# Attention scores from three bf16 parts in 32-wide tiles, with the masks of the transposed scores added by TensorE instead of selected by GpSimd

## The chip, the cores and the metric

The kernel runs on one core of a Trainium2 chip. The metric is the device time of one execution in microseconds, lower being better. The kernel before takes 4422.12 us (median of 3 runs, 4419.16 to 4424.13).

## The reference

One layer of a small language model over 32 sequences of 512 tokens, width 256, 16 heads of width 16. Every head attends twice: to keys at most 64 positions away, and to the first 64 keys of the sequence.

```python
h = take(emb_weight, x) + take(lora_A, x) @ lora_B.T * 2.0
n = layernorm(h)
q, k, v = split(n @ Wqkv + bqkv)                 # 16 heads of 16
s = q @ k.T / 4                                   # 512 x 512 of a head
attn_local  = softmax(where(abs(i - j) <= 64, s, -inf)) @ v
attn_global = softmax(q @ k[:64].T / 4) @ v[:64]
gate = sigmoid(n @ Wg + bg)
h = h + ((1 - gate) * attn_local + gate * attn_global) @ Wout + bout
n = layernorm(h)
# 8 experts, top 2 by softmax(n @ router_w.T), capacity 5121 rows of an expert
out = h + n + sum over the kept pairs of prob * (silu(n @ w1[e]) @ w2[e])
```

## The kernel before, in words

The program has a preparation, an attention stage (some 60 per cent of the time) and an expert stage, which the change leaves alone.

The attention stage goes through the sequences in turns. Turn i does the scores, exponentials and outputs of sequence i (`cur`), the projections of sequence i+1 (`nxt`), the embedding of i+2 (`far`), and the mixing, output projection and second layernorm of i-1 (`prev`); the routing of i-2 is in it too. Turns -2 to 3 and 30 to 34 are written out, turns 4 to 29 are one hardware loop (`turns`, L432). All engines follow one list of stages that `order` makes of 20 slots n = 0 to 19 and the tables `BEFORE` and `AFTER`; an engine skips the stages it has no part in, and each engine is in order.

A sequence has four quarters g of four heads, and each quarter five tiles: four of local scores (r = 0 to 3: a pair of heads by half a sequence) and one of global scores (r = 4). Slot n holds one tile of each of two kinds:

- `score_tile` (L715, L721) makes scores transposed, keys on partitions, queries along the row, in `psS[:, 0:2]`. ScalarE exponentiates them into `pl` or `pg` (L882, L886). GpSimd then sets what lies outside the band to zero (stage `sel`, L532 and L534), and `out_group` (L741, L746) multiplies by the values V.
- `max_tile` (L684, L696) makes scores the other way round in `psS[:, 2:4]`, adds the mask to them by a matmul of the identity with `mask` (L689), and VectorE takes the negated maxima of the rows (L970, L974) into `negm`. It works 9 slots ahead.

The maxima of a quarter go to `score_tile` as extra rows of Q against rows of ones in K, so that the subtraction is part of the matmul. Stage `m_rows` does that: TensorE transposes `negm` (L787), ScalarE and VectorE split it in two fp32r parts (L915, L1081), SyncE writes them to `m_scr` (L599), waits, and reads them into Q (L602). `score_tile` waits for this at the first tile of a quarter (slots 0, 5, 10, 15).

Precision comes from splitting: q and k are an fp32r high part and the rest (`qk_hi`, `qk_lo`, L941 and L1087), written three times to `qk_scr` (hi, lo, hi against hi, hi, lo), so one matmul contracts 48 rows, and two heads lie at partitions 0 and 64. SyncE's queue is in order too: in a turn it does load(i,3), m_rows(i,1), the load of `hb`, qk_write(i+1, 0), qk_write(i+1, 1) (L617), load(i+1,0) (L630), m_rows(i,2), load(i+1,1), m_rows(i,3), load(i+1,2), m_rows(i+1,0) and the stores of `held`, x2 and h. load(i+1,0) waits until all of qk_scr has landed.

## Time and profile before

| what | value |
|---|---|
| median of 3 runs | 4422.12 us |
| the profiled execution: time, span | 4414.52 us, 4412.8 us |
| share of the span that the engines are busy | PE 90%, DVE 56%, POOL 48%, ACT 41% |
| granted TensorE clock over the span | 0.902 of full speed |
| HBM read and written | 199.60 MB, 193.93 MB |

PE is TensorE's matmuls, PEld its weight loads, DVE VectorE, ACT ScalarE, POOL GpSimd, SP SyncE. The busy time of PE overlaps from one matmul to the next, since they are pipelined; what a group of matmuls costs is read from the start of the first to the start of what follows. A granted clock of 1.00 is 2.4 GHz, of 0.50 it is 1.2 GHz. An idle time stands with the work that ended it and what that work had waited for.

### The profile page before, as it was taken

Reading aid. Unit: us, or ns where it says so; the run is one execution under the profiler, and the core shown is the slowest. Engines: PE = TensorE matmul, PEld = TensorE weight load, DVE = VectorE, ACT = ScalarE, POOL = GpSimd, SP = SyncE. Lnnn points to the kernel's source line nnn. Section 1 sums busy time; section 2 is a strip of 40 time slices with the busy share of each in tenths; the row PEclk is TensorE's granted clock in tenths of the full one; section 3 lists DMA queues with packets and bytes.
Section 4 is the critical chain, followed back from the end, with each engine's and each line's share of the span. In section 5 each row is a group of like instructions: output and inputs, shape, how many; then the busy total and the mean of one; then the engine's idle time right before and its main releaser. Section 6 shows DMA issues by size and latency. Waiting matters only on the chain. (4 is left out here: it accounts for less than half of the span.)

```text
span 4412.8 us, 92560 instructions
## 1 busy us (share of the span) xinstructions
PE 3959.8 (90%) x31089; PEld 2974.9 (67%) x31090; DVE 2479.8 (56%) x5316; ACT 1830.4 (41%) x2933; POOL 2110.7 (48%) x2332
## 2 busy tenths in 40 slices
PE   2898989989989989998989987599999999999998
PEld 1455555555555555555555554599999999999998
DVE  3567676676677677667677674333343444334333
ACT  0344444444444444444444443344343444344343
POOL 2344555555555455455455444444444444444444
PEclk8798898898898898988888887799999999999999
DMA  5443443443443444444444431323232333322222
GB/s 125 99 130 101 113 131 92 113 129 101 105 128 102 111 122 106 126 103 113 121 100 113 126 97 41 98 46 65 46 68 45 65 58 56 64 46 48 44 44 41
DMA packets 243562, 395.27 MB, mean 90 GB/s; under 512 B 38533, under 2 KB 149589, under 8 KB 243317
## 3 DMA queue, kind: packets, MB, share of 16 engines
q1 hardware_dynamic: 170980, 301.18, 25.5%
q0 software_dynamic: 70512, 91.16, 12.0%
q8 instruction: 80, 1.31, 0.1%
q10 hardware_dynamic: 1952, 1.31, 0.1%
q14 instruction: 38, 0.30, 0.0%
HBM read 199.60 MB, written 193.93 MB: 89 GB/s over the span
## 5 line engine op out<-in xcount | busy, mean ns | idle before, releaser
L1344 POOL DMA_INDIRECT out_y<-out_t,tok_out x264 | 425.5, 1612 | 771.7 <-DMA out_y<-out_t,tok_out 410.0
L970 DVE TENSOR_REDUCE negm<-psS 128x4 f32<-128x1024 f32 x512 | 623.1, 1217 | 262.5 <-PE psS L689 260.0
L1552 DVE TENSOR_TENSOR h_lo<-act,h_hi 128x512 fp32r<-128x512 f32 x528 | 367.5, 696 | 583.5 <-ACT h_hi L1491 576.0
L1490 ACT ACTIVATE act<-psS 128x512 f32<-128x512 f32 x528 | 316.5, 600 | 911.0 <-PE psS L1418 899.1
L532 POOL TENSOR_SCALAR_AFFINE_SELECT pl<-pl 128x512 f32<-128x512 f32 x512 | 328.4, 641 | 757.6 <-ACT pl L882 757.3
L882 ACT ACTIVATE pl<-psS 128x896 f32<-128x896 f32 x512 | 468.3, 915 | 375.2 <-PE psS L715 373.0
L1453 PE MATMUL psO<-w_hi,h_hi 128*128 128x256 f32 x2112 | 598.9, 284 | 1.0 <-DVE h_lo L1552 0.9
L1453 PE MATMUL psO<-w_lo,h_hi 128*128 128x256 f32 x2112 | 588.8, 279 | 0.0
L1453 PE MATMUL psO<-w_hi,h_lo 128*128 128x256 f32 x2112 | 587.7, 278 | 0.0
L1418 PE MATMUL psS<-xg_hi,w_hi 128*128 128x256 f32 x1984 | 551.8, 278 | 0.1
L1418 PE MATMUL psS<-xg_hi,w_lo 128*128 128x256 f32 x1984 | 551.4, 278 | 0.0
L1418 PE MATMUL psS<-xg_lo,w_hi 128*128 128x256 f32 x1984 | 551.3, 278 | 0.0
L1453 PEld LDWEIGHTS psO<-w_hi,h_hi 128*128 128x128 f32 x2112 | 397.1, 188 | 1.6 <-DVE h_lo L1552 1.6
L1453 PEld LDWEIGHTS psO<-w_lo,h_hi 128*128 128x128 f32 x2112 | 397.0, 188 | 0.0
L1453 PEld LDWEIGHTS psO<-w_hi,h_lo 128*128 128x128 f32 x2112 | 395.5, 187 | 0.0
L1418 PEld LDWEIGHTS psS<-xg_hi,w_hi 128*128 128x128 f32 x1984 | 375.0, 189 | 0.3 <-issue 0.3
L1418 PEld LDWEIGHTS psS<-xg_lo,w_hi 128*128 128x128 f32 x1984 | 372.5, 188 | 0.0
L1418 PEld LDWEIGHTS psS<-xg_hi,w_lo 128*128 128x128 f32 x1984 | 372.5, 188 | 0.0
L715 PEld LDWEIGHTS psS<-Q,K 52*128 52x128 f32 x2048 | 171.5, 207 | 276.1 <-ACT pl L882 126.0
L689 PE MATMUL psS<-mask,identb 128*128 128x512 bf16 x1024 | 357.6, 436 | 0.0
L715 PE MATMUL psS<-Q,K 52*128 52x256 f32 (+1 forms) x2048 | 276.0, 351 | 76.9 <-ACT pl L882 59.0
L1584 DVE TENSOR_SCALAR out_t<-psO,wt_all 128x256 f32<-128x256 f32 x264 | 127.8, 484 | 367.8 <-PE psO L1453 362.9
(219 smaller groups left out, 7829.8 us busy)
## 6 DMA issues: line engine op xcount, KB each, us to landing
qk_scr<-qk_hi SPq DMA_DIRECT2D x128, 512.0 KB
Q<-qk_scr SPq DMA_DIRECT2D x256, 192.0 KB
K<-qk_scr SPq DMA_DIRECT2D x256, 192.0 KB
qk_scr<-qk_lo SPq DMA_DIRECT2D x64, 512.0 KB
h_rows<-held SPq DMA_DIRECT2D x32, 512.0 KB
hb<-h_rows SPq DMA_DIRECT2D x32, 512.0 KB
x_rows<-x SPq DMA_DIRECT2D x32, 512.0 KB
out_y<-h SPq DMA_DIRECT2D x32, 512.0 KB
```

Of the source, the lines that this page charges most:

```text
L532: pool.affine_select(out=cols[:, :, 0:P], in_=cols[:, :, 0:P], compare_op=ALU.is_ge, fill=0.0, base=0, pattern=[[0, 4], [1, P]], channel_m ...
L689: last = pe.matmul(psS[:, 2 + a, :], identb[:, :], mask[:, half, :, :], start=False, stop=True, skip_group_check=True)
L715: last = pe.matmul(psS[:, a, j % 2 * WIN + lo:j % 2 * WIN + hi], K[rows, 2 * g + v, j * P:(j + 1) * P], Q[rows, 2 * g + v, j * P - 64 + lo ...
L882: act.activation(pl[:, v, half, :, lo:hi], psS[:, 0:2, lo:hi], ACT.Exp, scale=SCALE).then_inc(exp_done, 1)
L970: dve.tensor_reduce(negm[:, g, 0, :, v, 2 * half:2 * half + 2], psS[:, 2:4, :].rearrange("p a (q u) -> p a q u", u=WIN), AX.X, ALU.max, ne ...
L1344: pool.indirect_dma_start(out=y[:, :], in_=out_t[:, tile.out, s, :], in_offset=None, out_offset=bass.IndirectOffsetOnAxis(ap=tok_out[:, ti ...
L1418: last = pe.matmul(psS[:, f // 2, (f % 2) * 256:(f % 2) * 256 + cols], w[:, tile.par, k, fs], x[:, k, 0:cols], start=(k == 0 and n == 0), ...
L1453: last = pe.matmul(psO[:, s, 0:D], h_[:, f, ts], w[:, tile.par, f, :], start=(f == 0 and n == 0), stop=(f == FT - 1 and n == 2))
L1490: act.activation(act32[:, b, :, 0:cols], src, ACT.Silu)
L1552: dve.tensor_tensor(h_lo[:, 2 * b:2 * b + 2, 0:cols], act32[:, b, :, 0:cols], h_hi[:, 2 * b:2 * b + 2, 0:cols].bitcast(F32), ALU.subtract) ...
L1584: dve.tensor_scalar(out_t[:, tile.out, s, :], psO[:, s, 0:D], wt_all[:, bass.ds(tile.h0 + s, 1)], None, ALU.mult).then_inc(out_done, 1)
```

## The change

q and k are cut in three bf16 parts instead of two fp32r ones: `qk1` by ScalarE, the rest in fp32 by VectorE, `qk2` by ScalarE (new stage `qk2`), `qk3` by GpSimd (new stage `qk3`). Six products of parts are kept, so a matmul contracts 96 rows and holds one head; with the maxima, in three parts also, 102 rows. The maxima are cut by VectorE before they are transposed (new stage `cut`), and m_rows comes later in its slot. Local scores are made in tiles of 32 rows of the result by 160 columns: each lands in 32 of the 128 PSUM partitions. `max_tile` adds the mask only where the band's corners are, and VectorE's maximum reads 160 columns of a block instead of 256. `score_tile` adds `mask_t` to the whole tile by matmuls with 32-wide pieces of the identity, and the stage `sel` of GpSimd is gone. The bias of the output projection is added in PSUM by one bf16 matmul per bank, and the copy `held` = h + bias on GpSimd is gone. Scratch takes about the same bytes in as many stores and half as many loads.

```diff
 # max_tile on TensorE
-                                lo, hi = edges(q)
                                 for a in range(2):
-                                    rows = slice(64 * a, 64 * a + ROWS)
-                                    pe.matmul(psS[:, 2 + a, q % 2 * WIN + lo:q % 2 * WIN + hi],
-                                              Q[rows, 2 * g + v, q * P:(q + 1) * P],
-                                              K[rows, 2 * g + v, q * P - 64 + lo:q * P - 64 + hi],
+                                    for c in range(4):
+                                        key = (4 * q + c) * SUB - SIDE
+                                        lo, hi = max(0, -key), min(BAND, T - key)
+                                        pe.matmul(psS[SUB * c:SUB * (c + 1), 2 + a, q % 2 * BAND + lo:q % 2 * BAND + hi],
+                                                  Q[0:ROWS, 4 * g + 2 * v + a, (4 * q + c) * SUB:(4 * q + c + 1) * SUB],
+                                                  K[0:ROWS, 4 * g + 2 * v + a, key + lo:key + hi],
...
-                                last = pe.matmul(psS[:, 2 + a, :], identb[:, :], mask[:, half, :, :], start=False, stop=True,
+                                for c in range(4):
+                                    last = pe.matmul(out[SUB * c:SUB * (c + 1), :, 0:5:4, :], identb[:, SUB * c:SUB * (c + 1)],
+                                                     tri[:, :, 0:5:4, :], start=False, stop=True, skip_group_check=True)
 # score_tile on TensorE
-                                    last = pe.matmul(psS[:, a, j % 2 * WIN + lo:j % 2 * WIN + hi],
-                                                     K[rows, 2 * g + v, j * P:(j + 1) * P],
-                                                     Q[rows, 2 * g + v, j * P - 64 + lo:j * P - 64 + hi],
-                                                     start=True, stop=True, skip_group_check=True)
+                                    for c in range(4):
+                                        key = (4 * j + c) * SUB
+                                        lo, hi = max(0, SIDE - key), min(BAND, T - key + SIDE)
+                                        pe.matmul(psS[SUB * c:SUB * (c + 1), a, j % 2 * WIN + SUB * c + lo:j % 2 * WIN + SUB * c + hi],
+                                                  K[0:ALL, 4 * g + 2 * v + a, key:key + SUB],
+                                                  Q[0:ALL, 4 * g + 2 * v + a, key - SIDE + lo:key - SIDE + hi],
+                                                  start=(j % 2 == 0), stop=False, skip_group_check=True)
+                            for j in range(2):
+                                for a in range(2):
+                                    for c in range(4):
+                                        pe.matmul(psS[SUB * c:SUB * (c + 1), a, j * WIN:j * WIN + SUB * (c + 1)],
+                                                  identb[:, SUB * c:SUB * (c + 1)], mask_t[:, 0:SUB * (c + 1)],
+                                                  start=False, stop=True, skip_group_check=True)
+                                    for c in range(4):
+                                        last = pe.matmul(psS[SUB * c:SUB * (c + 1), a, j * WIN + P + SUB * c:(j + 1) * WIN],
+                                                         identb[:, SUB * c:SUB * (c + 1)], mask_t[:, P + SUB * c:WIN],
+                                                         start=False, stop=True, skip_group_check=True)
 # out_group on TensorE
-                            pe.wait_ge(sel_done, SELECTS * s + 4 * g + 2 * (k + 1))
+                            pe.wait_ge(exp_done, JOBS * s + 5 * g + 2 * (k + 1))
 # GpSimd
-                            if stage == "sel":
...
-                                pool.affine_select(out=cols[:, :, 0:P], in_=cols[:, :, 0:P], compare_op=ALU.is_ge, fill=0.0,
...
+                            if stage == "qk3":
+
+                                pool.wait_ge(qk2_done, 4 * nxt + arg + 1)
...
+                                pool.tensor_tensor(qk3[:, arg, :], qk_rest[:, arg, :], qk2[:, arg, :], ALU.subtract).then_inc(qk3_done, 1)
 # SyncE, qk_write: each part of q (then of k) is waited for and written by itself
+                        for term, (rows, made) in enumerate(((qk1, qk1_done), (qk2, qk2_done), (qk3, qk3_done))):
+                            sp.wait_ge(made, 4 * s + 2 * (part + 1))
 # VectorE
-                            dve.tensor_reduce(negm[:, g, 0, :, v, 2 * half:2 * half + 2],
-                                              psS[:, 2:4, :].rearrange("p a (q u) -> p a q u", u=WIN),
+                            dve.tensor_reduce(negm[:, g, 0, v, :, 2 * half:2 * half + 2],
+                                              psS[:, 2:4, 0:2 * BAND].rearrange("p a (q u) -> p a q u", u=BAND),
 # the table AFTER, for one
-                5: (("cur", "out", 1), ("prev", "mix", 0), ("past", "top", 3)),
-                6: (("cur", "out", 2), ("prev", "mix", 1), ("past", "top", 4)),
+                5: (("cur", "out", 1), ("prev", "mix", 0), ("nxt", "qk3", 2), ("nxt", "qk3", 3), ("past", "top", 3)),
+                6: (("cur", "m_rows", 2), ("cur", "out", 2), ("prev", "mix", 1), ("past", "top", 4)),
```

How it moves instructions, at two places of the loop's turn. On TensorE, slot 6 before (the wait and transposes of m_rows(2), then a score tile and a max tile, then the output group and mixing):

```order
L787 MATMUL psX<-ident,negm 8x128 x4
L80 REGISTER_ALU
L715 MATMUL psS<-Q,K 128x192 x2
L715 MATMUL psS<-Q,K 128x256 x2
L684 MATMUL psS<-K,Q 128x192 x2
L684 MATMUL psS<-K,Q 128x256 x2
L689 MATMUL psS<-mask,identb 128x512 x2
L746 MATMUL psO<-pg,V 32x512 x4
```

and the same slot now, from the end of its score tile on; of that tile the last rows stand here. The numbers behind a name are partitions and columns of the result.

```order
L755 MATMUL psS<-mask_t,identb 32x32
L86 REGISTER_ALU
L702 MATMUL psS<-K,Q 32x96
L702 MATMUL psS<-K,Q 32x128
L702 MATMUL psS<-K,Q 32x160 x2
L702 MATMUL psS<-K,Q 32x96
L702 MATMUL psS<-K,Q 32x128
L702 MATMUL psS<-K,Q 32x160 x10
L709 MATMUL psS<-mask,identb 32x32 x2
L718 MATMUL psS<-mask,identb 32x2x2x32 x8
L825 REGISTER_ALU
L547 REGISTER_ALU
```

The score tile ahead of it went from 4 matmuls to 16 of scores (L744) and 32 of masks (L751, L755); the max tile went from 6 to 26; m_rows(2) (L828) now comes behind both. In one turn of the loop the program held 436 matmuls on TensorE before, and holds 1470 now.

On GpSimd, slots 5 and 6 before (`attn` is the sum of mix(0); the selections follow):

```order
L550 DMA emb_t<-in_L_tok_emb_weight,id_cur 128x256
L80 ISA
L566 ISA [waits attn_t_ready]
L567 TENSOR_TENSOR attn<-mix 128x256 [waits o_read]
L529 REGISTER_ALU
L532 AFFINE_SELECT pl<-pl 128x4x128 [waits exp_done]
L534 AFFINE_SELECT pl<-pl 128x4x128
```

and now (`qk<-qk_rest,qk` is qk3 from qk_rest and qk2):

```order
L573 DMA emb_t<-in_L_tok_emb_weight,id_cur 128x256
L86 ISA
L589 ISA [waits attn_t_ready]
L590 TENSOR_TENSOR attn<-mix 128x256 [waits o_read]
L594 REGISTER_ALU
L597 TENSOR_TENSOR qk<-qk_rest,qk 128x512 [waits qk2_done]
L594 REGISTER_ALU
L597 TENSOR_TENSOR qk<-qk_rest,qk 128x512 [waits qk2_done]
```

The last two cuts of k stand behind the sum of mix(0), which waits for VectorE's mixing; all of qk_write(i+1, 1) on SyncE waits for them.

## Rows read from the trace of the kernel before

**Rows 1.** Busy times in the loop of the attention stage and the expert stage

```profile
535.60:2585.00 2049.40, 1855.14 (x13911) 0.87 0.43 113
2830.00:4412.00 1582.00, 1532.38 (x13123) 0.98 0.30 54
```

**Rows 2.** TensorE at full clock: start, duration, engine, line, operation

```profile
1521.42 0.97 PE L696 MATMUL psS<-K,Q 48*128 48x64 f32 x16
1522.33 0.96 PE L741 MATMUL psO<-pl,V 128*32 128x256 f32 x16
1523.22 1.99 PE L773 MATMUL psX<-wv_sb,xn_t 128*128 128x256 f32 x8
...
1525.59 0.50 PE L715 MATMUL psS<-Q,K 52*128 52x192 f32 x4
1525.92 0.40 PE L684 MATMUL psS<-K,Q 48*128 48x192 f32 x4
1526.25 0.60 PE L689 MATMUL psS<-mask,identb 128*128 128x512 bf16 x2
1526.79 0.64 PE L746 MATMUL psO<-pg,V 128*32 128x512 f32 x4
```

**Rows 3.** TensorE at half clock, the same columns

```profile
1504.89 0.79 PE L715 MATMUL psS<-Q,K 52*128 52x192 f32 x4
1505.48 0.63 PE L684 MATMUL psS<-K,Q 48*128 48x192 f32 x4
1506.04 0.99 PE L689 MATMUL psS<-mask,identb 128*128 128x512 bf16 x2
1506.96 1.06 PE L746 MATMUL psO<-pg,V 128*32 128x512 f32 x8
```

**Rows 4.** Timeline of TensorE, small bf16 matmuls one behind another

```profile
1566.60 0.17 PE L865 MATMUL psX<-before,onesb 128*128 128x8 bf16 x1
...
1566.76 0.17 PE L865 MATMUL psX<-before,onesb 128*128 128x8 bf16 x1
```

**Rows 5.** Who waited for whom on TensorE in 25 turns: us, times, longest

```profile
PE psS L696 <- DVE negm L970: 58.4, 23, 2.9
...
PE psS L715 <- DMA Q<-m_scr: 8.6, 15, 0.9
```

**Rows 6.** Timeline of all engines around the rows of quarter 2

```profile
1549.18 0.73 POOL L567 TENSOR_TENSOR attn<-mix 128x256 f32<-128x256 f32 x1 [10.11 <-DVE mix L1056]
...
1551.90 0.32 SPq L630 DMA_DIRECT2D Q<-qk_scr  x1
...
1554.16 0.28 SPq L599 DMA_DIRECT2D m_scr<-m_hl  x1
...
1558.86 0.59 SPq L602 DMA_DIRECT2D Q<-m_scr  x2
...
1561.02 0.50 PE L715 MATMUL psS<-Q,K 52*128 52x192 f32 x4 [0.49 <-DMA Q<-m_scr]
...
1563.88 1.08 PE L696 MATMUL psS<-K,Q 48*128 48x64 f32 x16 [2.36 <-DVE negm L970]
```

**Rows 7.** Groups by line: count, busy us, mean ns of one, idle before

```profile
L970 DVE TENSOR_REDUCE negm<-psS 128x4 f32<-128x1024 f32 x512 | 623.1, 1217 | 262.5 <-PE psS L689 260.0 <-issue 1.1
...
L573 POOL TENSOR_TENSOR held<-h,bout_b 128x1024 f32<-128x1024 f32 x32 | 75.4, 2355 | 41.1 <-DVE h L1132 41.1
```

**Rows 8.** DMA queues, 120 to 600 us: packets, MB, share

```profile
q8 instruction: 22, 0.36, 0.3%
```

**Rows 9.** DMA queues, 600 to 2500 us, all that were in use

```profile
q1 hardware_dynamic: 114673, 200.53, 39.5%
q0 software_dynamic: 13280, 13.03, 3.2%
```

**Rows 10.** TensorE around a jump in the expert stage

```profile
3014.52 0.28 PE L1453 MATMUL psO<-w_hi,h_lo 128*128 128x256 f32 x1
3020.96 0.58 PE L1418 MATMUL psS<-xh_hi,w_hi 128*128 128x256 f32 x1 [6.16 <-issue]
```

More of the change, by code:

```diff
@@ L719, in score_tile @@
                         else:
                             for v in range(2):
-                                last = pe.matmul(psS[:, v, :], KG[:, 2 * g + v, :, :], Q[:, 2 * g + v, :], start=True, stop=True)
+                                for a in range(2):
+                                    last = pe.matmul(psS[64 * a:64 * (a + 1), v, :], KG[0:ALL, 4 * g + 2 * v + a, :],
+                                                     Q[0:ALL, 4 * g + 2 * v + a, :], start=True, stop=True, skip_group_check=True)
```

288 lines of the change are left out of this document (162 added, 126 removed).

## The prediction

> **What bounds the kernel now.** First the busy times by stretch [rows 1]. In the 25 turns of the loop that this window spans, TensorE is busy 1855 of 2049 us, and a turn takes 82.0 us; idle time is 7.8 us a turn. No other engine comes near in the table above. So the attention stage is TensorE's, at a mean granted clock of 0.87: about a quarter of it runs at 1.2 GHz, the rest at 2.4. The expert stage is busier still, and the change does not touch it. Then the waits of the same stretch [rows 5]: 58.4 us, 2.3 a turn, is the global max tile L696 waiting for VectorE's previous maxima, and 8.6 us, 0.34 a turn, is a score tile waiting for its rows from `m_scr`. What a tile costs TensorE is read from starts in the timeline, since busy times overlap.
>
> **TensorE, tile by tile.** At full clock [rows 2] a local score tile takes 1525.92 - 1525.59 = 0.33 us and a local max tile 1526.79 - 1525.92 = 0.87 us, of which the two mask matmuls of 512 bf16 columns are 0.54 (0.53 ns a column). A slot's pair is 1.20. At half clock [rows 3] it is 0.59 + 1.48 = 2.07, the masks 0.92 for 1024 columns, 0.90 ns each.
>
> Now the pair is 48 + 26 = 74 matmuls. They land in four strips of 32 partitions, and what the strips cost side by side is the question. The nearest row is L741 [rows 2]: 16 records of fp32, four strips, per strip 2 x (256 + 192) = 896 columns of records, in 1523.22 - 1522.33 = 0.89 us, 0.99 ns a column. The full-width fp32 matmuls behind it (8 records of 256 columns, up to about 1525.1) take 0.9 a column, so four strips run as one. A bf16 column costs half an fp32 one by the same rows (0.53 against 0.9 to 1.0); I take 0.50. Per strip the score tile streams 4 x 160 of scores and 4 x 160 of masks, 1280 columns, 0.64 us; the max tile 4 x 160 + 2 x 32 + 2 x 128 = 960 columns, 0.48 us. The pair is 1.12 at full clock, 15 ns a matmul, and 2240 x 0.90 = 2.02 at half. Gain 0.08 us by 16 pairs, -1.3 us a turn. The score tile gets dearer and the max tile cheaper; they cancel almost.
>
> The four global max tiles take 0.91 each now, from L696 to L741 [rows 2], 57 ns a matmul, bound by their weight loads (64 columns are soon streamed). In bf16 the nearest row is the chain L864/L865 with the same 128-wide bf16 weights: seven starts, six steps, in 0.16 us, 27 ns [rows 4]. 16 x 27 = 0.43, so -0.48 by 4 = -1.9. Transposing the maxima in bf16: 16 matmuls of 128 columns at 0.53 instead of 0.9, -0.8; the bias adds two of 512 columns, +0.5. Together -3.5 at full clock. At half clock the fp32 parts save twice that, so I take **-4.0 us a turn**. The global score tiles stream what they did (two strips of 64, 512 columns, twice).
>
> **The waits.** The maximum reads 640 elements a partition instead of 1024; L970 takes 1217 ns [rows 7], in proportion some 0.4 us less, so VectorE sheds over 6 us a turn and gets four short cuts (`cut`) for L1081. The wait of 2.3 us at L696 (2.36 of it in one turn) [rows 5, 6] has half a dozen other things of VectorE in front of it; I let 2.0 of it go and 0.5 of the shorter ones: **-2.5**. The selections lie on GpSimd, and TensorE hardly waits for them, so their removal is worth nothing by itself; the cover is the distance between a score tile and its output group. `held` likewise. The new `qk2` (ScalarE, behind VectorE's rest) delays exponentials 4 and 5 by 1 to 1.5 us, which the projections on TensorE (3.6 us each pair) and the mixing cover; uncovered it would cost that.
>
> **What is late next: the rows of quarter 2.** The score tile of slot 10 started at 1561.02, 0.49 us late for these rows [rows 6], so this chain is already on the path. It is: the last part of k, the stores to `qk_scr`, all landed at 1551.90, load(i+1,0), the store L599 at 1554.16, the load L602 at 1558.86, landed at about 1561. The change puts the last two cuts of k on GpSimd behind the sum L567, which ended at 1549.91. A cut of 128x512: a sum over 1024 takes 2355 ns [rows 7], over 256 it is 0.73 [rows 6], so 1.27 us between. Two end at 1552.5. The last store (a sixth of the bytes) then has little ahead of it; a small transfer and its signal take some 2 us in this chain (1558.86 to 1561), so all has landed at about 1554.6 instead of 1551.9, +2.7. Two loads are issued instead of four, which gives back 1 us. The rows come 1.1 to 1.7 us later, while TensorE, whose work before slot 10 shrinks by about 2, would come earlier. So slots 5 to 9 give back their 2 and lose 1 more: **+3.0 us a turn**. GpSimd, relieved of selections, is not late before L567, whose releaser is the mixing.
>
> **The program's length.** TensorE runs 556 matmul records a turn (13911 in 25 [rows 1]), each with a weight load. The loop's body goes from 436 to 1470 matmuls of the program, so to 556 + 1034 = 1590 pairs. In the written-out turns the instruction queue q8 brought 22 packets in 480 us [rows 8], one for some 20 us; in the loop neither it nor any other instruction queue appears [rows 9]: the body of 4 or 5 packets was kept. In the expert stage, where the body is longer, TensorE sat idle for 6.16 us at a jump between experts, with nothing that it waited for [rows 10]. A jump of the turns' loop is bounded by nothing and 6.16; at that place between experts the program jumps more than once, so I take the middle, 3.1. At the end of a turn TensorE has the value matmuls queued (8 records are about 1.9 us by [rows 2]), which covers more than half. With a body of 12 or 13 packets that is not kept I take **+1.5** a turn.
> The Trainium skill (Runtime: NRT & Kernel Launch, "Instruction fetch mechanics") says that TensorE's buffer holds 2048 instructions and that a taken branch out of it forces a fetch before execution goes on. By that rule the old body of some 1200 fits and the new one of over 3200 does not, and the stall appears; the trace agrees as far as [rows 9, 10] show; the sum without the stall would be 39 us lower.
>
> **Sum.** A turn of the loop: -4.0 - 2.5 + 3.0 + 1.5 = -2.0; 26 turns, -52. The six other whole turns have no jump: -3.5 each, -21. The preparation gets about 2 us of bias cutting ahead of the lora copies: +2. In all -71 from 4414.5 us, the profiled execution's own time, which is 7.6 below the median; 4343.5 to 4351, and I say **4347**.
>
> **The rivals.**
> *Small matmuls cost by number (slower).* If a 32-wide matmul cannot follow another faster than the 27 ns of [rows 4], a pair costs 74 x 27 = 2.0 instead of 1.12: +0.88 by 512 pairs = +450 us, of which waits would swallow perhaps a tenth: about 4750. It decides at 71/512 = 0.14 us a pair, 17 ns a matmul, only 2 ns above my price; 20 ns give 4347 + 0.36 x 512 = 4530. For it: the chain of [rows 4], and a longer program to be fetched and dispatched. Against it: L741, where 16 records and 16 loads pass in 0.89 us at the rate of their columns; but those have 56 ns each to hide in. Chance 0.25.
> The Trainium skill (TensorE: Matmul & The Clock Gate, "Wait — 56ns, not 53.3ns?") gives a floor of about 25 ns from one matmul's start to the next, which makes this case; its Part 3 on row and column tiling puts matmuls of different strips 4 ns apart, which makes mine. No row here shows such short ones in strips.
> *Instructions come too slowly (slower).* If the jump costs all of 6.16 us and nothing is queued, or packets are awaited inside the turn too, +4.7 a turn or more: 4347 + 26 x 4.7 = 4470. For it: [rows 10], and dense slots take 150 instructions in little over 1 us. Against it: 13 packets a turn are one for 6 us. Chance 0.15.
> *The chain of quarter 2 stays hidden (faster).* If the last cuts come earlier, or the rows' transfer is faster without the four loads ahead of it, the +3.0 falls away: -3 x 32 = -96, 4250. Against it: it is already 0.49 late. Chance 0.18.
> *My forecast*, 4300 to 4400: 0.42.
>
> **How the numbers follow.** 0.2 per cent, 9 us, is what a measurement of this kernel can tell from no change. Faster holds the forecast's and the third rival's chance, less a little at the upper edge: 0.57. Same is the narrow strip between forecast and instruction rival: 0.07. Slower: 0.36. The range 4240 to 4560 leaves out the far half of the small-matmul case and the low tail beyond 4240; its cost bounds are 15 to 20 ns a small matmul and 0 to 6.2 us a jump.
>
> **What would show it.** Right: L702 plus its masks 0.45 to 0.55 us from start to start at full clock, L744 with L751 and L755 0.6 to 0.7; L724 in about 0.45; the wait for negm at L724 mostly gone; a wait of 3 to 4 us for Q from m_scr at slot 10; q8 at 12 or 13 packets a turn all through the loop with an idle of 1 to 2 us "issue" near the turn's start. Wrong: a pair of tiles at over 1.3 us, idle time put down to issue in the middle of a turn, a mean clock in the loop more than 0.03 away from 0.87, or no wait at slot 10.

## The result, and the profile after

The changed kernel takes 4647.56 us (median of 4), the kernel before 4421.92 beside it. One of the four runs, 5744 us at a granted clock of 0.63, was in a slow state and is left out of the ratio, which is 1.0506, 95% interval 1.0485 to 1.0526. It is 5 per cent slower, where I had forecast 1.5 per cent faster.

First the windows of the changed kernel (length, TensorE's busy time with its records, granted clock, DMA share, GB/s, as in [rows 1]): 24 turns of the loop, and the expert stage.

```profile
529.80:2718.50 2188.70, 1786.92 (x38159) 1169.76 (x38160) 1093.18 (x3192) 925.82 (x1369) 613.59 (x623) 0.87 0.35 103
3060.00:4642.00 1582.00, 1528.28 (x13073) 1526.41 (x13070) 626.27 (x1227) 657.99 (x1206) 729.55 (x547) 0.98 0.30 53
```

A turn takes 2188.70 / 24 = 91.2 us instead of 82.0. TensorE's busy time is the same, 74.5 us against 74.2, at the same clock of 0.87; its idle time went from 7.8 to 16.7. The expert stage is as it was. So the whole loss is idle time in the turns of the loop. The waits of TensorE in those 24 turns say what kind (total, times, longest), to be held against [rows 5]:

```profile
PE psX L828 <- DVE m_cut L1043: 109.2, 49, 3.5
PE psS L744 <- issue: 84.7, 27, 5.5
PE psO L782 <- issue: 45.8, 77, 1.5
PE psS L702 <- issue: 40.0, 42, 1.5
PE psS L724 <- issue: 29.8, 66, 1.1
PE psS L755 <- issue: 26.9, 58, 0.5
```

"Issue" is idle time in which TensorE waited for no engine and no transfer that the profile shows: 258 us over all lines, 10.7 a turn. Before it had next to none: in a stretch of 1600 us its rows add up to 6.5 us, those of the changed kernel to 194.3. The wait for negm is down from 58.4 us to 0.2, as forecast, and a new one has come, 4.5 us a turn, for the last step of VectorE's cut.

The tiles' prices held. The timeline at full clock, against [rows 2]:

```profile
1515.99 0.46 PE L744 MATMUL psS<-Q,K 102*32 102x160 bf16 x16
...
1516.57 0.45 PE L702 MATMUL psS<-K,Q 96*32 96x160 bf16 x15
```

The score tile with its masks takes 1516.57 - 1515.99 = 0.58 us, and the max tile, to 1517.10, 0.53: the pair 1.11 against 1.12 forecast, 15 ns a matmul. In front of an output group (L782) the same pair takes 0.95 (1521.09 to 1522.04), 13 ns a matmul: what a tile costs depends a little on what follows it. The global max tile takes 0.57 where I had 0.43. VectorE's reduction, to [rows 7]:

```profile
L1019 DVE TENSOR_REDUCE negm<-psS 128x4 f32<-128x640 f32 x512 | 420.1, 820 | 553.4 <-PE psS L718 388.2 <-remote 164.7
```

Now the two kinds of "issue". In the queues of the same loop (packets, MB, share) there is an instruction queue, where [rows 9] had none, with 14 packets of 16 KB a turn, and the jump back is followed by a stall:

```profile
q1 hardware_dynamic: 110995, 197.36, 31.0%
q0 software_dynamic: 13212, 12.99, 2.9%
q8 instruction: 322, 5.28, 1.1%
```

```profile
1547.52 0.72 PE L744 MATMUL psS<-Q,K 102*32 102x96 bf16 x16 [4.12 <-issue]
```

The second kind stands in mid-turn. TensorE and GpSimd in the timeline of the changed kernel:

```profile
1499.43 1.00 POOL L581 DMA_INDIRECT slot_table<-entry,slot_i  x1 [0.17 <-issue]
...
1500.73 0.98 POOL L581 DMA_INDIRECT slot_table<-entry,slot_i  x1 [0.30 <-issue]
1500.74 0.26 PE L751 MATMUL psS<-mask_t,identb 128*32 128x96 bf16 x2 [0.54 <-issue]
...
1501.51 0.21 PE L755 MATMUL psS<-mask_t,identb 128*32 128x96 bf16 x3 [0.48 <-issue]
...
1502.02 0.97 POOL L581 DMA_INDIRECT slot_table<-entry,slot_i  x1 [0.30 <-issue]
1502.25 0.37 PE L724 MATMUL psS<-K,Q 96*128 96x64 bf16 x4 [0.31 <-issue]
...
1503.01 0.24 PEld L724 LDWEIGHTS psS<-K,Q 96*128 96x128 bf16 x4 [0.55 <-issue]
```

Some eight instructions, about four loads with their matmuls, start every 0.74 us and nothing in between, and this goes on for 3 to 9 us. It happens some 45 us after the jump, while GpSimd issues its eight scatters of a turn 1.3 us apart. The clock follows. Windows of one turn: behind the jump, a good stretch, the slow stretch, and what comes after it (the last figures: granted clock, DMA share, GB/s).

```profile
1547.50:1556.50 9.00, 8.98 (x180) 6.21 (x182) 2.80 (x6) 2.90 (x4) 0.00 (x0) 0.70 0.02 4
1583.50:1592.50 9.00, 7.47 (x254) 5.46 (x253) 7.34 (x23) 4.02 (x6) 5.15 (x6) 1.00 0.53 117
1592.50:1600.50 8.00, 4.80 (x34) 1.91 (x35) 0.00 (x0) 0.00 (x0) 5.85 (x6) 0.58 0.32 83
1600.50:1609.50 9.00, 7.94 (x191) 5.56 (x190) 4.07 (x13) 5.41 (x8) 0.00 (x0) 0.99 0.03 7
```

The granted clock is 0.70 behind the jump, 0.58 in the slow stretch, 1.00 and 0.99 around it.

Last, the cut of quarter 2, VectorE and GpSimd:

```profile
1576.61 0.17 DVE L1034 CAST m_cut<-negm 128x32 bf16<-128x32 f32 x1
...
1576.93 0.48 DVE L1037 TENSOR_TENSOR m_rest<-negm,m_cut 128x32 f32<-128x32 f32 x1
1577.33 2.26 POOL L597 TENSOR_TENSOR qk<-qk_rest,qk 128x512 bf16<-128x512 f32 x2
1577.56 0.95 DVE L1040 CAST m_cut<-m_rest 128x32 bf16<-128x32 f32 x1
1578.66 0.98 DVE L1043 TENSOR_TENSOR m_cut<-m_rest,m_cut 128x32 bf16<-128x32 f32 x1
...
1579.77 0.34 PE L828 MATMUL psX<-identb,m_cut 128*24 128x128 bf16 x3 [3.53 <-DVE m_cut L1043]
```

The last two steps take 0.95 and 0.98 us while the sum `qk3` runs on GpSimd. Over the whole trace the last step takes 973 to 976 ns in the 30 of 128 cases with such a sum beside it, and 191 to 194 in the other 98.

### The profile page after: what moved, and what is told of

Same layout as the page of the kernel before. It is cut to its first block and busy times, and to the rows that moved or that the text cites. A ratio compares the mean times of both kernels' runs of the same rounds, so it can differ in the third digit from the quotient of the medians.

```text
span 4642.9 us, 157324 instructions
## 1 busy us (share of the span) xinstructions
PE 3937.7 (85%) x64177; PEld 3118.3 (67%) x64178; DVE 2143.7 (46%) x5594; ACT 1918.2 (41%) x3061; POOL 1570.1 (34%) x1413
## 5 line engine op out<-in xcount | busy, mean ns | idle before, releaser
L1019 DVE TENSOR_REDUCE negm<-psS 128x4 f32<-128x640 f32 x512 | 420.1, 820 | 553.4 <-PE psS L718 388.2
L782 PE MATMUL psO<-pl,V 128*32 128x192 f32 (+1 forms) x4096 | 361.2, 401 | 55.2 <-issue 53.0
L597 POOL TENSOR_TENSOR qk<-qk_rest,qk 128x512 bf16<-128x512 f32 x128 | 147.4, 1171 | 763.6 <-ACT qk L991 763.6
L744 PE MATMUL psS<-Q,K 102*32 102x160 bf16 (+2 forms) x8192 | 264.6, 247 | 135.0 <-issue 93.8
L744 PEld LDWEIGHTS psS<-Q,K 102*32 102x32 bf16 x8192 | 158.9, 102 | 309.4 <-issue 232.1
L601 POOL TENSOR_TENSOR h<-h,x 128x1024 f32<-128x1024 f32 x32 | 75.2, 2351 | 786.6 <-DVE x L1214 786.6
```

Of the source, the lines that this page charges most:

```text
L597: pool.tensor_tensor(qk3[:, arg, :], qk_rest[:, arg, :], qk2[:, arg, :], ALU.subtract).then_inc(qk3_done, 1)
L601: pool.tensor_tensor(h1[:, :, :], h1[:, :, :], x2[:, :, :], ALU.add).then_inc(res_done, 1)
L744: pe.matmul(psS[SUB * c:SUB * (c + 1), a, j % 2 * WIN + SUB * c + lo:j % 2 * WIN + SUB * c + hi], K[0:ALL, 4 * g + 2 * v + a, key:key + SU ...
L782: last = pe.matmul(psO[32 * c:32 * (c + 1), 0, j * P - 64 + lo:j * P - 64 + hi], V[:, j, 4 * g + c, :], pl[:, c // 2, k, c % 2, j % 2 * WI ...
L1019: dve.tensor_reduce(negm[:, g, 0, v, :, 2 * half:2 * half + 2], psS[:, 2:4, 0:2 * BAND].rearrange("p a (q u) -> p a q u", u=BAND), AX.X, A ...
```

## The experiments

Times are medians; "before" ran on the same chip each time, at 4408 to 4419 us. Differences between runs of different groups are good to some 10 us. Theory A: the loop body is no longer kept, so that the jump stalls. B: small matmuls cost by their number. C: the wait for the cuts. D: GpSimd's bursts of indirect transfers (gathers and scatters whose rows are picked by an index) slow the supply of instructions. Where an expectation gives a loop body 3360, 1966 or 1710 instructions, the traces, from jump to jump, hold 3267, 1864 and 1608 records of TensorE, loads and matmuls counted apart.

### The jump

```diff
+                    with pe.Fori(2, SEQ // 2 - 1) as m:        # in the kernel before, TensorE alone
+                        for s in range(2):
+                            turn(2 * m + s, whole(4))
```


> The kernel BEFORE, with one edit: TensorE's loop holds two turns in its body and goes round 13 times instead of 26; the other engines and all of the work are as before. The body grows from some 1200 to some 2400 instructions, no matmul is added. Theory A (the changed kernel is slow because its loop body is no longer kept, so that each jump back stands still for 4 to 7 us and instructions arrive late in between): the queue q8 appears in the loop, the 13 jumps take 4 us or more each, and the time rises by 13 x 4.5 = 58 us to about 4480 (4460 to 4500); no idle put down to issue in mid-turn, since this kernel issues only 1200 instructions in 82 us. Theory B (the many small matmuls cost by their number) and theory C (TensorE waits for the new cuts of the maxima): unchanged, 4422 within 9.

Measured 4468.07 against 4419.41: ratio 1.0118 (1.0096 to 1.014). 13 jumps, 49 us, 3.7 us each, and q8 appears with 124 packets between 620 and 2500 us. No matmul was added, so B has no part in it.

```diff
-                    turns(pe, turn)                              # in the changed kernel
+                    for i in range(-2, SEQ + 3):
+                        turn(i, dict(old=0 <= i - 3 < SEQ, ...))
```


> The CHANGED kernel, with one edit: TensorE's turns are all written out, so TensorE makes no jump in the attention stage; the other engines keep their loops. Theory A in two parts: the jump (3.5 us of idle a turn) goes, 26 x 3.5 = -91 us; the late instructions in mid-turn (7 us a turn) stay, if they are a matter of the rate at which new instructions can be had: about 4555 (4530 to 4580), q8 at 14 packets a turn as now. If the jump alone does it and the mid-turn idle is its after-effect, all 10.7 us a turn go: about 4370. Theory B: 4648, unchanged, as theory C has it.

Measured 4552.9: 95 us less, 3.6 us a jump, as the first part of A has it. The mid-turn idle stayed: "issue" still adds up to 132.6 us in 1600, with no jump left.

### Fewer instructions

```diff
-                                    for c in range(4):           # score tile: 16 matmuls and 32 masks
-                                        pe.matmul(psS[SUB * c:SUB * (c + 1), a, ...
+                                    last = pe.matmul(psS[:, a, j % 2 * WIN + lo:j % 2 * WIN + hi], ...   # 4 matmuls
+                                pool.affine_select(out=cols[:, :, 0:P], ...        # as before the change
```


> The CHANGED kernel with the local score tiles 128 wide again (4 bf16 matmuls of up to 256 columns instead of 16 of 160) and with the two selections by GpSimd instead of the 32 mask matmuls; the max tiles stay 32 wide with their masks on TensorE. TensorE's loop body is 44 x 2 x 16 = 1408 instructions shorter: 1952 instead of 3360. Theory A: if some 2000 instructions are kept, q8 is gone from the loop, the jump is 0.2 us, and the 10.7 us of issue idle a turn go; with a score tile of 4 x 256 x 0.53 ns / 1.27, at most 0.50 us, instead of 0.58 another 1.3 to 2.6 us: 26 x 12.5 + 6 x 6 = -360, about 4290 (4240 to 4340), faster than both kernels. If the body is still too long: the jump stays, about 4380. Theory C alone: the wait of 4.5 us a turn at the transposes of the maxima stays in full, so that most of the loss against the kernel before stays: 4560 or more.

> The CHANGED kernel with only the masks of the score tiles taken from TensorE and given back to GpSimd's two selections; the score tiles stay 32 wide (16 matmuls). TensorE's loop body is 32 x 2 x 16 = 1024 instructions shorter: 2336 instead of 3360. Theory A, with a limit near 2000 instructions: the jump stays at 4 us or so, q8 brings some 9 packets a turn, the mid-turn idle of 7 us a turn shrinks with the number to 3 to 4, and the mask matmuls' own time goes, 16 x 0.29 = 4.6 us a turn: 32 x 8 = -255, about 4390 (4350 to 4440). If 2336 instructions are still kept: about 4280, near the kernel with wide score tiles. Theory B (the price is by number, the jump is no matter): the saving is in proportion to the matmuls, 512 of 1634 a turn, and so the same 4.6 us a turn and no more: 4500.

a_wide_select: 4426.01, ratio to before 1.0012 (0.9998 to 1.0027). a_strip_select, with the 16 small score matmuls kept: 4396.98, 0.9947 (0.9927 to 0.9966). The second is where it was expected. The first was expected at 4290, or at 4380 if its body was still too long, and missed both. Its body of 1864 TensorE records is not kept: q8 brings 200 packets in 1880 us and the jumps stall as before. And its waits lie elsewhere:

```profile
PE psX L830 <- DVE m_cut L1045: 115.4, 56, 3.2
PE psS L756 <- issue: 48.3, 32, 4.7
PE psS L716 <- DVE negm L1021: 45.5, 25, 2.7
PE psS L738 <- DVE negm L1021: 17.5, 19, 1.0
```

Cuts and maxima cost it 115 + 63 us in 1600. It has no slow stretches. That the kernel with 12 matmuls more a tile is the faster one speaks against B once more.

### The scatters

```diff
+                    if on["cur"] and 0 < n < 4 * QB:             # order(): a_paced_scatters has 2 * QB <= n
+                        yield "pace", n
+                            if stage == "pace":                  # GpSimd
+                                pool.wait_ge(exp_done, JOBS * i + arg)
```


> The CHANGED kernel, with one edit: before each of GpSimd's slots 1 to 15 it waits for the exponential of the slot before, as the selections made it do. The gathers and the eight scatters of a turn then go out one a slot instead of back to back; nothing else changes. Theory D: eight indirect transfers that GpSimd starts back to back slow the supply of TensorE's instructions. In the changed kernel, in 18 of 18 turns, TensorE gets some eight instructions every 0.74 us for 2 to 9 us (84 us in 1600), and only while GpSimd issues scatters 1.3 us apart. By D most of it goes: 4 us a turn, 32 x 4 = -128, about 4520 (4490 to 4560). Theory A' (the mid-turn idle is a matter of the number of instructions alone): 4648 within 10. A third possibility, that each single scatter costs as much as one in the burst: unchanged too, with the trickle spread over eight slots.

> The CHANGED kernel; GpSimd waits for the exponential of the slot before in slots 8 to 15 alone, where the scatters stand, and not in slots 1 to 7, where the gathers do. a_paced, with both, measured 4294 against 4648. Theory D (the burst of eight scatters holds up TensorE's instructions): nearly all of the gain is here too, 4294 to 4340. If the gathers share in it in proportion to their number, half: about 4470. If pacing acts in another way (through the sums of q and k or of the mixing, which now run at other times), anything above 4340.

a_paced: 4293.61, ratio to before 0.9734 (0.9714 to 0.9753), 354 us less than the changed kernel and faster than the kernel before. a_paced_scatters: 4298.68, so the scatters hold all of it. I had expected 128. Windows and waits of a_paced:

```profile
700.00:2300.00 1600.00, 1372.80 (x32265) 934.20 (x32267) 933.63 (x2700) 776.68 (x1155) 519.94 (x529) 0.93 0.39 118
```

```profile
PE psX L833 <- DVE m_cut L1048: 90.2, 40, 3.5
PE psS L749 <- issue: 61.2, 20, 4.6
PE psS L749 <- ACT pl L931: 18.1, 33, 1.1
PE psS L707 <- issue: 16.0, 13, 1.5
```

A turn is 78.9 us. "Issue" fell from 11.1 to 4.5 us a turn. The rest is busy time, from 74.5 to 67.7 us a turn with the same work, at a granted clock of 0.93 for 0.87; in proportion the clock would give 4.8 of that (an estimate). The selections had paced GpSimd before; with them went the pacing.

Is it the burst that does it? Counted in the traces, from 620 to 2500 us: gaps of 0.55 to 1.5 us between the starts of two successive matmuls of one line, in the score and max tiles.

| kernel | gaps | of these within 2 us after GpSimd issues an indirect transfer | share of the time in such stretches |
|---|---|---|---|
| changed | 134 | 117 | 0.27 |
| a_written_out | 161 | 133 | 0.28 |
| a_rows_later | 19 | 1 | 0.30 |
| a_paced | 9 | 0 | 0.38 |
| a_paced_scatters | 13 | 0 | 0.35 |
| a_paced_written | 10 | 3 | 0.36 |
| a_paced_written_3 | 113 | 99 | 0.34 |
| a_paced_all_3 | 5 | 0 | 0.39 |
| b_no_select | 34 | 9 | 0.30 |
| b_no_select_two | 34 | 7 | 0.30 |
| a_short_burst | 1 | 0 | 0.32 |
| a_short_burst_two | 0 | 0 | 0.31 |

The gaps of the two b kernels are no slow supply: they lie no oftener behind a transfer than elsewhere, and nearly all are at the global score tile (L708), whose matmuls are 512 columns wide; the kernel before has 29 of them.

Four runs ask what a burst needs. Two have the kernel before's tiles, without selections, with a kept and with a fetched body. They leave the masks of the score tiles out altogether, so they do less than the whole work:

```diff
-                                pool.affine_select(...)          # both, in the kernel before
-                            pe.wait_ge(sel_done, SELECTS * s + 4 * g + 2 * (k + 1))
+                            pe.wait_ge(exp_done, JOBS * s + 5 * g + 2 * (k + 1))
```


> The kernel BEFORE without GpSimd's two selections a score tile (so the local scores are not masked in the second pass: this work is left out); output groups wait for the exponentials instead. GpSimd's scatters then go out back to back, as in the changed kernel, while TensorE's loop body of 1206 records is kept and nothing is fetched. Theory D1 (the burst holds up the fetching of instructions from memory): no trickle of instructions here, 4412 less the few waits for selections, so 4390 to 4425, and no idle put down to issue over 0.5 us at the scatters. Theory D2 (the burst holds up TensorE's issue whatever the source of its instructions): idle at the scatters, clock down, some +20 to +60 us.

> The kernel of b_no_select (4306; the second pass's masks are left out) with TensorE's loop body holding two turns, as in b_two_turns: instructions are now fetched all through, while the eight scatters go out back to back. In b_no_select, with a kept body, the scatters held nothing up. Theory D1 (a burst of scatters holds up the FETCHING of instructions): +52 us for 13 jumps as in b_two_turns, and beside it idle put down to issue at the scatters, 1 to 4 us a turn with the clock falling there: 4306 + 52 + 26 to 100, so 4385 to 4460. Against it (the burst does nothing to the fetch, and the slow stretches of the changed kernel come from its own rate of instructions alone): 4306 + 52 = 4358, within 12, and no such idle.

b_no_select: 4305.78, ratio 0.9754 (0.9738 to 0.977). There is no slow stretch at its bursts; but it is 105 us faster, which no theory had (the lowest expectation was 4390). b_no_select_two: 4371.4, 66 us more, of which 49 are the 13 jumps by b_two_turns. The other 17 lie between the two expectations, and the trace shows no idle put down to issue at the scatters (16.8 us in 1600, at the jumps). So a burst beside a fetched program is not enough, if few instructions are wanted.

Two more have the 32-wide max tiles and a burst, again with a kept and with a fetched body (a_wide_select with the mask edit of a_short_later, and without selections, so again without the masks of the score tiles):

> The kernel of a_short_later with m_rows in its first slots again and without GpSimd's selections (the second pass's masks are left out). Max tiles are 32 wide (16 small matmuls and 2 wide), score tiles have 4 matmuls; the body of some 1710 records should be kept, and the scatters go out back to back. D1 (the burst holds up fetching): no gaps beyond a handful inside a tile at the scatters, no row of issue over 10 us in 1600. D2 (it holds up TensorE's issue of small matmuls whatever their source): 50 or more gaps of 0.4 us and more within 2 us after a scatter, and the clock below 0.90. Time by D1 some 4150 to 4250, by D2 50 to 150 more.

> The same with TensorE's loop body holding two turns, so that the same instructions are fetched. D1: gaps at the scatters appear here and only here, and the time rises by the 49 us of 13 jumps and 30 to 200 more. D2: gaps in both, and +49 us within 15. If neither kernel has gaps, small tiles of this density are not enough, or do not meet the burst, and the two are not told apart.

4158.68 (ratio 0.9414, 0.9394 to 0.9435) and 4214.17 (0.9534, 0.9508 to 0.956): 56 us for 13 jumps, and at the scatters no idle put down to issue in either, and one gap or none. With 22 matmuls a slot the burst does nothing, with the 74 of the changed kernel it does. Fetching and issuing are not told apart by this.

The instruction queue's packets in the trace say something on it. In the changed kernel a packet of 16 KB that starts while the scatters of a turn go out takes 1.09 us in the median and at most 1.36, like the others (1.11); in a_paced, which has no slow stretches, those packets take 1.62. Only 23 of the 134 gaps fall while a packet is under way, and half of them end 2.7 us or more after the last one has landed, although a packet holds some 230 records. So the slow stretches are not slow packets.

What changed in b_no_select is seen on VectorE, in groups from 700 to 2300 us (count, busy us, mean ns): first the kernel before, then b_no_select.

```profile
L1095 DVE CAST KG<-K 48x128 fp32r<-48x128 f32 x156 | 78.6, 504 | 1.1
L1164 DVE TENSOR_SCALAR xn<-h,mv,rstd 128x256 f32<-128x256 f32 x76 | 75.6, 1053 | 0.7
...
L1009 DVE TENSOR_TENSOR before<-before,chosen 128x8 bf16<-128x8 bf16 x76 | 33.6, 443 | 2.0
```

```profile
L1082 DVE CAST KG<-K 48x128 fp32r<-48x128 f32 x164 | 48.7, 297 | 1.1
...
L1151 DVE TENSOR_SCALAR xn<-h,mv,rstd 128x256 f32<-128x256 f32 x80 | 28.3, 416 | 0.7
...
L996 DVE TENSOR_TENSOR before<-before,chosen 128x8 bf16<-128x8 bf16 x84 | 13.4, 159 | 2.2
```

The scaling of xn falls from 1053 to 416 ns, the copy of the keys from 504 to 297, the routing's sums from 443 to 159, and `coef` from 398 to 192: with 4, 8, 4 and 4 of them a turn, 6.2 us. The trace of the kernel before shows the same within one kernel. The routing's sum takes 153 ns with nothing on GpSimd beside it and 612 beside a selection (28 and 48 cases), `coef` 192 and 605, the scaling 400 alone, 718 beside selections and 1965 beside selections and a GpSimd sum. The copy of the keys takes 241 alone and 2289 in the 20 cases beside the mixing's sum and a selection. So the selections slow VectorE, in part by the sums that they push into its way. That this is what makes the kernel 105 us faster is argued, not shown. TensorE's idle time for the maxima falls from 56 us in 1600 to 13, but waits for rows and for the start of other work come in its place. In a turn 3.3 us shorter (78.7 us for 82.0) its idle time falls by only 0.5, and its busy time by 2.8, from 74.2 to 71.4.

### The cuts and the rows

```diff
-                6: (("cur", "m_rows", 2), ("cur", "out", 2), ...
+                7: (("cur", "m_rows", 2), ("prev", "mix", 2)),   # and so 1 -> 2, 11 -> 12, 16 -> 17
```


> The CHANGED kernel, with one edit: the transposes of the cut maxima (m_rows) stand one slot later on TensorE and ScalarE, in slots 2, 7, 12 and 17 instead of 1, 6, 11 and 16; VectorE's cuts stay where they are. Theory C: TensorE waits 4.5 us a turn there for VectorE's cut, which a slot of other work would hide: up to -4.5 a turn, 32 x 3.5 to 4.5 = -110 to -145, about 4520. Rival: VectorE is late as a whole at these places (behind the mixing and the rests of q and k), and the same idle is found at the next max tile or at the mixing, or the score tile of slot 5, 10, 15 or 0 now waits for its rows: 4620 to 4660.

> The kernel of a_wide_select (4426) with m_rows one slot later. It lost 6.1 us a turn to the wait for the cuts. Theory C: 32 x 4 to 6 = -130 to -190, about 4270. Rival (VectorE is late anyway): the waits for the maxima grow by what this one loses, 4400 or more.

> The CHANGED kernel with both edits: GpSimd paced (a_paced, 4294) and the transposes of the maxima one slot later (a_rows_later, 4378). The two faults are different waits. If they add: the wait for the cuts, 4.4 us a turn in a_paced, goes, and 1 to 2 us come back as the wait for the rows in slot 10: 32 x -2.5 = -80, about 4215 (4190 to 4250). If the rows of quarter 2, 3.6 us late at worst in a_rows_later, take it all back: 4280 or more.

a_rows_later: 4378.44, ratio 0.9898 (0.9855 to 0.9942). a_wide_select_later: 4278.55, 0.9693 (0.9677 to 0.9709), 147 us less than a_wide_select. a_paced_later: 4322.33, 0.9785 (0.9761 to 0.9808), 29 us more than a_paced. The same edit thus gains 269, gains 147 and loses 29. The first is not the cut's alone: the slow stretches are gone too (19 gaps for 134), although the scatters still go out 1.3 us apart. Nor is TensorE away from small tiles at that time: from a turn's first scatter to 2 us after its last, 12.9 us, it starts 180 matmuls of 32 columns of weights on average, where the changed kernel starts 84 in 12.8 us. So a burst and small tiles side by side are not enough for a slow stretch. The waits of a_rows_later:

```profile
PE psS L744 <- issue: 54.3, 21, 4.1
PE psS L744 <- DMA Q<-m_scr: 49.9, 19, 3.6
PE psS L744 <- ACT pl L926: 36.3, 32, 2.3
PE psS L702 <- DVE negm L1019: 32.1, 21, 1.6
PE psX L852 <- ACT m_t L958: 31.0, 20, 2.5
```

The wait for the cut is gone, and 49.9 us, 19 times, are the rows of quarter 2 at slot 10.

```diff
-                5: (..., ("prev", "mix", 0), ("nxt", "qk3", 2), ("nxt", "qk3", 3), ...
+                6: (..., ("prev", "mix", 1), ("nxt", "qk3", 2), ("nxt", "qk3", 3), ...
```


> a_paced with GpSimd's last two sums qk3 in slot 6 behind the mixing instead of in slot 5. In all kernels so far VectorE's last step of the cut of quarter 2 takes 975 ns while such a sum runs on GpSimd (30 of 30) and 192 ns otherwise (98 of 98), and the cut of quarter 2 ends 3 us after it began. If the two engines' sharing is the cause: that step back at 193 ns, the wait for the cut in slot 6 down from 3.5 to 1 to 1.5 us, 32 x -2 = -65, about 4230, if the later stores to qk_scr (by 3 to 4 us) do not make the score tile of slot 10 wait. If they do, 4290 or more, with a wait for Q from m_scr or qk_scr in slot 10. If the sharing is not the cause, the step stays at 975 ns.

Measured 4483.31, ratio 1.0154 (1.0107 to 1.0201), 190 us more than a_paced. The last step of the cut is at 193 ns in all 128 cases, and the longest wait for it falls from 3.5 to 2.0 us: that part is right. The price is larger:

```profile
PE psS L749 <- DMA Q<-m_scr: 158.8, 19, 9.6
PE psX L833 <- DVE m_cut L1048: 57.9, 37, 2.0
```

```profile
1506.20 0.33 SPq L652 DMA_DIRECT2D Q<-qk_scr  x1
1506.57 0.42 SPq L652 DMA_DIRECT2D K<-qk_scr  x1
1507.24 0.29 SPq L625 DMA_DIRECT2D m_scr<-m_t  x1
1512.49 0.26 SPq L627 DMA_DIRECT2D Q<-m_scr  x1
```

SyncE's queue: the two loads of quarter 0, the store of the rows behind them, and their load only 5.3 us later. The score tile of slot 10 waits up to 9.6 us.

### Versions without the faults

```diff
-                                    for c in range(4):           # a_short_later: a_wide_select_later, and in the max tile
-                                        ... identb[:, SUB * c:SUB * (c + 1)], tri[...]
+                                last = pe.matmul(psS[:, 2 + a, 0:2 * BAND]..., identb[:, :], mask[:, half, :, :], ...)
```


> The kernel of a_wide_select_later with the ten mask matmuls of a max tile replaced by two of 128 x 320 columns. The loop body goes from 1966 to 1710 records of TensorE. Where the limit is a buffer of some 2000 instructions of which the fetch ahead takes a part, 1710 may be kept: then q8 is gone from the loop, the jump is 0.2 us, and 26 x 2.5 to 4 = -65 to -100 us against a_wide_select_later, less +0.1 us a max tile, 51 us at most: about 4240. If it is not kept: the same as a_wide_select_later or up to 40 us more.

> The CHANGED kernel with GpSimd paced in slots 8 to 15 (a_paced_scatters, 4299) and TensorE's turns written out, so that both faults of the instruction supply are gone, the jump and the slow supply at the scatters. If they are two faults that add: another -26 x 3.5 = -91 us, about 4207 (4185 to 4230), with q8 still at 14 packets a turn. If the jump was partly hidden, or what it held up is now held up by the cuts: 4240 or more.

a_short_later: 4235.92, ratio 0.96 (0.9578 to 0.9621). Its body of 1608 records is kept: 7 instruction packets between 620 and 2500 us, 207 or 208 ns for the jump's instruction, no "issue" row. a_paced_written (a_paced_scatters with TensorE's turns written out): **4185.46, ratio 0.9495 (0.9477 to 0.9513)**, the fastest that does all of the work; the jumps, worth 95 us alone, give 113 here, beside the 349 of the scatters. Its window is to be held against [rows 1] and that of a_paced:

```profile
700.00:2300.00 1600.00, 1416.39 (x34224) 971.40 (x34216) 981.66 (x2863) 826.24 (x1230) 548.76 (x555) 0.94 0.42 125
```

A turn is 74.2 us: TensorE is busy 65.7 of it and idle 8.5, for 74.2 and 7.8 in the kernel before. The whole gain over the kernel before is thus in busy time, at a granted clock of 0.94 for 0.87.

> The kernel of a_paced_written (4185), with m_rows of quarters 1, 3 and 0 one slot later (slots 2, 12, 17) and that of quarter 2 where it was (slot 6). In a_paced_written TensorE waits 5.4 us a turn for the cuts, 3.5 of it at most at slot 6, and in a_paced_later moving all four brought a wait for the rows of up to 5.4 us and no gain. If the loss there was quarter 2's alone: the 2 us a turn of the other three cuts go without it, 32 x -1.5 = -50, about 4140. If the copy of the rows by ScalarE or the maxima behind it hold TensorE up in its place (they did for 1.7 and 1.5 us a turn in a_paced_later): 4185 to 4230.

> The kernel of a_paced_written_3 (4444) with GpSimd paced in slots 1 to 7 too, where the gathers stand, and not only in slots 8 to 15. In a_paced_written_3, 155 of 169 gaps of 0.4 to 1.5 us between two matmuls of one small tile lie within 2 us after an indirect transfer that GpSimd issued; such stretches are 34 per cent of the time. Many of these are now gathers, five of them back to back at the turn's end. Theory D in its wider form (indirect transfers issued back to back, gathers or scatters, hold up the fetch if small tiles are being run): those gaps at the gathers go, at least half of the 258 us come back, 4150 to 4310. Against it (the slots' new order is bad for another reason, a wait that moves): 4400 or more.

Moving three of the four transposes in it gave 4443.55 (ratio 1.0047, 1.003 to 1.0063), 258 us the wrong way: the gaps are back, 113 of them. 47 are within 2 us after a gather, five of which go out 1.3 us apart and which that kernel does not pace; 52 are after a scatter, and in 28 of these no other transfer had gone out in the 1.7 us before it. Pacing the gathers too gave 4233.15 (0.9591, 0.9566 to 0.9616) and 5 gaps. So 210 us hung on how GpSimd's gathers are spaced. But a_paced_written has the same 23 bursts of five gathers in this stretch, and 10 gaps. The remaining 48 us against a_paced_written are waits that moved, for the exponentials (50.3 us in 1600 for 15.6) and ScalarE's copy of the rows (36.4 us, which a_paced_written did not have).

## Why the prediction was wrong

**TensorE, tile by tile: right.** The pair costs 1.11 us, 15 ns a matmul, and the rival "small matmuls cost by number" is refuted by the timeline, and by a_strip_select, which has 12 matmuls more in a tile than a_wide_select and is faster (b_two_turns adds no matmul and says nothing on it). Only the global max tile is 0.14 dearer than its row in [rows 4] promised.

**The waits for the reduction: right.** -2.3 us a turn against -2.5.

**The program's length: the mechanism right, the size wrong.** I put the stall at 1.5 us a turn, the half of 3.1 being covered; b_two_turns gives 3.7, a_written_out 3.6, and the waits of the changed kernel 84.7 / 24 = 3.5. Nothing covered it. The Trainium skill (Runtime: NRT & Kernel Launch, "Instruction fetch mechanics") gives 2048 instructions for TensorE's buffer. The runs bound what a loop can use of it: bodies of 1206 and 1608 records in the trace are kept, one of 1864 is not, so it is somewhat less than that figure. The same section takes the fetch of straight code to be mostly hidden. In a_paced_written it was: 43.0 us in 1600, 2.0 a turn, are put down to issue. In a_written_out, the same straight code with the scatters in a burst, it is 132.6 us, 7.3 a turn.

**The step that failed: "the removal of the selections is worth nothing by itself".** It failed twice, with opposite signs. The selections slowed VectorE's instructions by 6.2 us a turn, and the kernel before without them gains 105 us. The Trainium skill (SBUF — State Buffer, "Who interferes with whom") has the rule, by which copies and scalings in a two-port mode, and instructions with two inputs from SBUF beside a GpSimd instruction that reads it, contend with GpSimd, and reductions never do. The rows agree: 975 for 193 ns in the cut, 1053 for 416 in the scaling, and 1216 for 1218 in the reduction. And the selections also spaced GpSimd's indirect transfers one a slot. I had looked at who waits for the selections, and not at what waits behind them. Without them the eight scatters go out back to back, and spacing them again gives 349 us (a_paced_scatters), more than the whole miss of 300.

**The rival "instructions come too slowly"** named the place, idle put down to issue in mid-turn, with a chance of 0.15 and 4470 us. It was 4648 because the supply fails in stretches, with the clock down in them (0.58), and not evenly.

**The rows of quarter 2: real, but hidden.** The +3.0 us a turn did not come: TensorE was late itself. With the cut's wait taken away they come, 49.9 us in 1600 or 2.6 a turn (a_rows_later), and with the last sums one slot later 158.8, or 8.5. What took their place was a wait that I had not priced, TensorE for `cut`, 4.5 us a turn: the transposes stand right behind the last maximum, and four dependent steps of VectorE had come between.

**What it adds up to.** In a_paced_written, without both faults of the supply, the change is worth 4185 - 4408 = -223 us. My sum without the stall was -71 - 39 = -110. The 105 us of b_no_select would fill the gap, but that match is not shown to be more than luck. Two of my terms were wrong in opposite ways there and nearly cancel: the rows' +3.0 did not come, and the wait for the cuts, 106.7 us in 1600 or 4.9 a turn, was not in the sum. And the gain over the kernel before is not idle time at all (8.5 us a turn for 7.8) but busy time, 8.5 us a turn, at a clock of 0.94 where I had kept 0.87 throughout. In proportion the clock alone makes 5.5 us a turn of it (an estimate: 74.2 x 0.87 / 0.94 = 68.7); the other 3 us are near the 3.5 at full clock that I had for the tiles. What raised the clock no run isolates.

What stays open: how GpSimd's indirect transfers slow the supply. Shown is that spacing them removes the slow stretches (a_paced, a_paced_scatters, a_paced_all_3), and that a burst does nothing where few matmuls are wanted (a_short_burst_two, b_no_select_two). Not shown is that burst and dense small matmuls together suffice: a_rows_later and the gathers of a_paced_written have both and next to no gaps. So a condition is missing, and it may be the moment in TensorE's program that the transfers meet, since moving the transposes by a slot took the stretches away once and brought them back once. The packets of the instruction queue are not slower in them. Whether what lies behind the packets or the issuing suffers, and whether from the transfers or from their making on GpSimd, no run tells: no kernel had so many small matmuls in a body that is kept.

## What to carry to other kernels

Count the instructions of a loop's body on each engine before making its tiles smaller: the price of a tile can be right and the kernel still lose by its supply. When work is removed from an engine that has time to spare, ask what it had been pacing and what it had been holding up, for both can be worth more than the work. And a short wait in one kernel can be the cover of another: the same move of the transposes was worth -269, -147 and +29 us.

## What the runs showed of the hardware

Four strips of 32 partitions took 74 bf16 matmuls with 74 weight loads in 0.95 to 1.11 us, 13 to 15 ns each. A TensorE loop of 1608 records ran all but without an instruction fetch (7 packets in 1880 us), one of 1864 with 9 packets a turn and up to 4.7 us of idle behind a jump. In the changed kernel, under a burst of indirect transfers from GpSimd, 1.3 us apart, the instructions of the small tiles came at about eight every 0.74 us, with the packets of the instruction queue no slower than elsewhere (1.09 for 1.11 us); in a_rows_later, under the same burst, they did not. TensorE's granted clock in such a stretch was 0.58, and of the 12.3 us a turn that pacing gave back, 5.5 were idle time and 6.8 busy time. A VectorE step of 32 columns took 975 ns beside a sum on GpSimd instead of 193, and a sum of 8 columns 612 ns beside a selection instead of 153.
